# One packed operand for the last half block of a shared expert's gate and up projections

## The reference

```python
F, FS = (176, 704)
shared = silu(x @ Wsg) * (x @ Wsu) @ Wsd        # Wsg, Wsu: 256 x 704, Wsd: 704 x 256
shared = shared * jax.nn.sigmoid(x @ Wse)
...
out = shared.at[tok].add(y_pair)
```

## Time and profile before

| | us |
|---|---|
| median of three runs | 497.82 |
| the profiled execution | 498.43 |
| its span in the trace | 496.7 |
| TensorE busy in the span | 470.5 (95%) |
| VectorE busy | 288.1 (58%) |
| ScalarE busy | 212.9 (43%) |
| GpSimd busy | 57.4 (12%) |

### The profile page before, as it was taken

One profiled execution on the slowest core, in us unless ns is written; L12 is line 12 of the kernel. 1 busy time (PEld: TensorE's weight loads), 2 busy tenths in 40 slices (PEclk: granted clock), 3 DMA queues, 4 the chain that ended last, 5 costly groups with the idle time before them and its releaser, 6 DMA issues.

```text
span 496.7 us, 8113 instructions
## 1 busy us (share of the span) xinstructions
PE 470.5 (95%) x3022; PEld 393.2 (79%) x3022; DVE 288.1 (58%) x713; ACT 212.9 (43%) x564; POOL 57.4 (12%) x91
## 2 busy tenths in 40 slices
PE   1999999899999999999999989999989899999997
PEld 1778888798888889898989779899866656557897
DVE  5536553656666666666666655665688853535111
ACT  3454630355555556555555666334253232231100
POOL 4050000000000000000000000011432168400000
PEclk9999999999999999999999999999999999999999
DMA  7900520101010010100000000000599159910001
GB/s 197 235 14 1 170 74 11 43 1 44 0 40 6 3 41 2 42 1 1 2 1 1 1 1 1 1 1 1 178 297 296 45 155 278 300 29 1 1 32 54
DMA packets 40439, 32.33 MB, mean 65 GB/s; under 512 B 6432, under 2 KB 38864, under 8 KB 40400
## 3 DMA queue, kind: packets, MB, share of 16 engines
q1 hardware_dynamic: 40400, 31.80, 23.2%
HBM read 30.75 MB, written 1.05 MB: 64 GB/s over the span
## 4 chain that ended last, share of the span: by engine, by line
PE 78%; DVE 11%; ACT 5%; issue 3%; DMA 1%; POOL 0%; SPq 0%; ACTq 0%; DVEq 0%; POOLq 0%
PE bank L771 13%; PE bank L772 12%; PE bank L773 12%; PE bank L913 4%; PE bank L1133 4%; PE bank L930 4%; PE bank L921 3%; PE bank L947 2%; PE bank L1105 2%; PE bank L931 2%; ACT arena L611 2%; PE bank L911 2%; PE bank L1064 2%; PE bank L1125 2%; PE bank L1171 2%
## 5 line engine op out<-in xcount | busy, mean ns | idle before, releaser
L609 ACT ACTIVATE arena<-bank,nmax 128x128 f32<-128x128 f32 x64 | 23.5, 368 | 92.6 <-DVE nmax L1315 92.6
L771 PE MATMUL bank<-XTl,WA 128*128 128x512 f32 x128 | 54.7, 427 | 4.4 <-DVE XTl L1218 3.6
L772 PE MATMUL bank<-XTh,WA 128*128 128x512 f32 x128 | 51.4, 402 | 0.0
L773 PE MATMUL bank<-XTh,WA 128*128 128x512 f32 x128 | 51.4, 401 | 0.0
L489 POOL TENSOR_TENSOR arena<-arena 128x256 f32<-128x256 f32 x20 | 16.7, 862 | 278.5 <-ACT arena L672 258.4
L1320 DVE RECIPROCAL rinv<-psumr 128x2 f32<-128x2 f32 x64 | 10.6, 166 | 61.1 <-ACT arena L611 60.9
L913 PE MATMUL bank<-arena 128*128 128x256 f32 x128 | 41.6, 407 | 0.0
L771 PE MATMUL bank<-WA,XTh 128*128 128x256 f32 x128 | 38.4, 300 | 0.0
L930 PE MATMUL bank<-arena 128*128 128x256 f32 x128 | 38.3, 381 | 0.0
L921 PE MATMUL bank<-ident,arena 128*128 128x128 f32 x192 | 32.5, 278 | 5.7 <-DVE arena L1323 5.7
L772 PE MATMUL bank<-WA,XTl 128*128 128x256 f32 x128 | 35.7, 279 | 0.0
(11 more groups left out here) (261 smaller groups left out, 1219.0 us busy)
## 6 DMA issues: line engine op xcount, KB each, us to landing
arena<-in_L_ffn_Wg SPq DMA_DIRECT2D x6, 704.0 KB, 8.4
arena<-in_L_ffn_Wu SPq DMA_DIRECT2D x6, 704.0 KB, 9.8
arena<-in_L_ffn_Wd SPq DMA_DIRECT2D x6, 512.0 KB, 7.5
arena<-in_L_attn_Wq SPq DMA_DIRECT2D x4, 512.0 KB, 6.5
arena<-in_L_attn_Wk SPq DMA_DIRECT2D x8, 256.0 KB, 2.7
arena<-in_L_attn_Wv SPq DMA_DIRECT2D x8, 256.0 KB, 3.2
arena<-in_L_attn_Wo SPq DMA_DIRECT2D x1, 2048.0 KB, 8.3
arena<-in_L_ffn_Wd SPq DMA_DIRECT2D x6, 192.0 KB, 8.0
```

Source lines behind the costliest of these rows:

```text
L609: nc.scalar.activation(Pb[:, i, 0:128], pb[i][:, 0:128], ACT.Exp, bias=nmax[:, i, 0:1], accum_out=psumr[:, i, 0:1])
L771: pe.matmul(dst, wh, xl, start=start, stop=False)
L772: pe.matmul(dst, wl, xh, start=False, stop=False)
L773: return pe.matmul(dst, wh, xh, start=False, stop=stop)
```

## The change

The half blocks of gate and up, 64 columns each, are laid side by side in one operand of 128 columns (`tail`), high and low. For block 5 `shared_up` runs once for both (k = 0 alone; with k = 1 only its waits are left), and its one bank holds the gate's result in partitions 0 to 63 and the up projection's in 64 to 127. `silu` reads the lower half and writes to partitions 64 to 127 of `ACTT[5]`; `shared_product` multiplies there. The last 64 rows of the down weights are loaded to partitions 64 to 127, and `shared_down` multiplies block 5 with those 64 rows only. With no padding left, its two memsets and their semaphores go; the DMAs that waited for them wait for what the memsets waited for. `SGR` has 704 columns for each part and no gap.

```diff
-        SGR = region(9728, 3072).rearrange("p (a c n) -> p a c n", a=2, c=C)
+        SGR = region(9728, 4 * FS).rearrange("p (a c n) -> p a c n", a=2, c=C)
...
+        def tail(part):
+            return SG[:, (FC - 1) % 2, part, 0].rearrange("p c (a n) -> p a c n", a=2)
...
-            sp.wait_ge(s_pd, 1)
+            sp.wait_ge(s_ol, 2 * NT)
...
-                    sp.wait_ge(s_ps, 1)
+                    sp.wait_ge(s_yh, 2 * NT)
...
-                    sp.dma_start(SD[0:FS - P * (FC - 1), FC - 1], a["L1_ffn_Wsd"][P * (FC - 1):FS, :]).then_inc(s_sd, 16)
+                    sp.dma_start(SD[P - FT:P, FC - 1], a["L1_ffn_Wsd"][P * (FC - 1):FS, :]).then_inc(s_sd, 16)
...
             pool.wait_ge(s_ol, 2 * NT)
-            pool.memset(SGR[:, :, :, FS:FP], 0.0).then_inc(s_pd, 1)
...
             pool.wait_ge(s_yh, 2 * NT)
-            pool.memset(SD[:, FC - 1], 0.0).then_inc(s_ps, 1)
...
             def g_high(m):
...
+                if m == FC - 1:
+                    nc.scalar.activation(tail(0), SGR[:, :, :, P * m:FS], ACT.Copy).then_inc(s_gh, 1)
...
             def silu(q):
...
+                if m == FC - 1:
+                    nc.scalar.activation(ACTT[m][P - FT:P, 512 * half:512 * half + 512], pb[up_bank(q)][0:FT], ACT.Silu).then_inc(s_ss, 1)
+                    return
...
             def shared_up(q, k):
...
+                if m == FC - 1:
+                    if k == 0:
+                        for c in range(C):
+                            ins = mm3(pb[up_bank(q)][:], SG[:, m % 2, 0, 0, c], SG[:, m % 2, 1, 0, c],
+                                      XTh[:, c, xs], XTl[:, c, xs], c == 0, c == C - 1)
+                        ins.then_inc(s_sf, 2)
+                    return
...
             def shared_down(j):
...
-                    ins = pe.matmul(pb[j % 4][:, 0:D], ACTT[m][:, P * j:P * j + P], SD[:, m], start=(m == 0), stop=(m == FC - 1))
+                    r = slice(P - FT if m == FC - 1 else 0, P)
+                    ins = pe.matmul(pb[j % 4][:, 0:D], ACTT[m][r, P * j:P * j + P], SD[r, m], start=(m == 0), stop=(m == FC - 1))
...
             def g_low(m):
...
+                if m == FC - 1:
+                    for i in range(2):
+                        ins = nc.vector.tensor_tensor(tail(1)[:, i], SGR[:, i, :, P * m:FS], tail(0)[:, i].bitcast(F32), ALU.subtract)
+                    ins.then_inc(s_gl, 1)
+                    return
...
             def shared_product(q):
...
+                if m == FC - 1:
+                    nc.vector.tensor_tensor(dst[P - FT:P], dst[P - FT:P], pb[up_bank(q)][P - FT:P], ALU.mult).then_inc(s_sm, 1)
+                    return
```

More of the change, by code:

```diff
@@ L43 @@
 FC = 6
-FP = FC * P
+FT = FS - P * (FC - 1)
 SLOTS = E1 * CAP
@@ L262, in program @@
         s_x1 = sem("x1_ready")
-        s_pd = sem("shared_up_padding_ready")
-        s_ps = sem("shared_down_padding_ready")
         s_pe = sem("expert_padding_ready")
@@ L400, in _ @@
                 load_kv(p)
-            sp.wait_ge(s_pd, 1)
+            sp.wait_ge(s_ol, 2 * NT)
             for i, n in enumerate(("Wsg", "Wsu")):
-                sp.dma_start(SGR[:, i, :, 0:FS], a["L1_ffn_" + n].rearrange("(c p) n -> p c n", p=P)).then_inc(s_sg, 16)
+                sp.dma_start(SGR[:, i], a["L1_ffn_" + n].rearrange("(c p) n -> p c n", p=P)).then_inc(s_sg, 16)
             sp.wait_ge(s_pe, 3)
@@ L676, in g_high @@
                     act.wait_ge(s_sf, 2 * shared.index((m - 2, 1)) + 2)
-                nc.scalar.activation(SG[:, m % 2, 0], SGR[:, :, :, P * m:P * m + P], ACT.Copy).then_inc(s_gh, 1)
+                if m == FC - 1:
+                    nc.scalar.activation(tail(0), SGR[:, :, :, P * m:FS], ACT.Copy).then_inc(s_gh, 1)
+                else:
+                    nc.scalar.activation(SG[:, m % 2, 0], SGR[:, :, :, P * m:P * m + P], ACT.Copy).then_inc(s_gh, 1)
             o_high(3)
```

## The result

The changed kernel takes 502.85 us (median of 6 runs, 501.84 to 505.45) against 497.78 us; the ratio is 1.0102 with a 95% interval of 1.0079 to 1.0124, so it is 5.1 us slower. The direction was forecast, the size was not: 500.4 us was predicted, with a range from 498.7 to 501.5.

A forecast was written before the change was run, and what follows sets the result against it. TensorE, busy 470.5 of 496.7 us, was taken as the bound, with VectorE holding `shared_down`. Terms -0.56 and +3.2 gave +2.6 us: 500.4 us on the median of 497.82, range 498.7 to 501.5.

The forecast's parts named there:

- The bound: TensorE bounds the kernel, but from 446.73 to 449.23 us VectorE's copy, masks and last product hold `shared_down`.
- the up pass of q 11: Six multiplications removed behind `down` 7; they ended before VectorE's last shared product began, so removal gains 0.
- The turn of the last group, 0.56 us: In `turn` 7 the second transpose starts 0.22 us behind VectorE's product, at 443.42 instead of 443.98: gain 0.56 us.
- VectorE's part, 2.50 us "and it stays": From the start of the copy of `down` 7 to `shared_down`, VectorE's work stays 2.50 us long.
- The switches, 3.2 us: In `shared_down`, sixteen changes between 128 and 64 rows cost 0.20 us each, adding 3.2 us.
- four early distances: Early trace rows where the used array part changes: each load comes 0.07 us before the record ahead's modelled end.
- rivals of free and of half-priced switches: `shared_down`'s row switches cost nothing (497.3 us, chance 0.07) or half (498.8 to 498.9 us, chance 0.06).
- The memsets, "0": Removing both padding memsets, at 352.38 us and on an idle GpSimd, gains 0; without cover 0.3 us each at most.
- The clock, left out of the sum, chance 0.05: Rival: about 2.5 us idle ahead of `shared_down` halves TensorE's rate for 3.4 us, costing 1.7 more: 502.1, chance 0.05.
- 1.32 us of idle time: TensorE's idle stretch ahead of 393.64 us, after which its row shows full rate; cited when weighing the clock rival.

The follow-up runs named there:

- e7: Kernel before, both passes kept, only the up pass of q 11 moved ahead of `down` 7: 496.79 us against 497.55, ratio 0.9982.
- e10: Changed kernel without the waits that the two dropped passes left on TensorE's queue: 504.6 us, one run.
- e1: Changed kernel, but `shared_down` multiplies block 5 with all 128 rows (zeros added): 498.73 us against 498.21 before, ratio 1.0015.
- e3: Changed kernel plus six unused multiplications filling TensorE's idle stretch ahead of `shared_down`: 501.94 us, ratio 1.0076 to the kernel before.
- e6: Changed kernel with the edits of e1, e4 and e10 together: 493.98 us against 497.55 before, ratio 0.9927.
- e8: e1 plus the six unused multiplications of e3 in the idle stretch: 497.63 us, ratio 0.9999 to the kernel before.
- e12: Changed kernel plus two tiny early GpSimd memsets of 8 unused columns each: 501.66 us, one run.
- e2: Kernel before, both up passes kept, only `shared_down` changed to multiply block 5 with rows 0 to 63: 501.24 us against 498.21, ratio 1.0067.
- e9: e4 with `shared_down`'s blocks descending for every second j, so 8 row switches instead of 16: 496.8 us against 497.94 before, ratio 0.997.
- e5: Changed kernel plus one GpSimd memset of 64 unused rows where the second padding memset was: 501.78 us, ratio 1.0079 to the kernel before.
- e11: Changed kernel plus one tiny early GpSimd memset of 8 unused columns: 502.08 us, one run.
- e4: Changed kernel with both packed passes of block 5 written ahead of `down` 7: 498.05 us, ratio 0.9998 to the kernel before.

## Why the prediction was wrong

*The bound.* Right: VectorE held `shared_down`, and the up pass of q 11 was worth nothing. e7 confirms it from the other side.

*The turn of the last group, 0.56 us.* The mechanism held, the size did not. The product ended at 443.94 and the second transpose started at 444.33, 0.39 us later and not 0.22. The waits of the dropped pass stay on TensorE's queue and are worked off only behind the product; in e10, without them, it is 0.22 (one run). The prediction put no price on them.

*VectorE's part, 2.50 us "and it stays".* It became 449.87 - 447.13 = 2.74. Before, the mask began 0.34 us behind the start of the copy and before the copy's end (VectorE's timeline; the chain in the earlier trace rows shows the time from the copy's end on):

```profile
447.07 1.41 DVE L1529 TENSOR_SCALAR GT<-FRF,slot_t 128x1024 fp32r<-128x1024 f32 x2
```

Now the mask begins 0.46 us behind it, when the copy is over, and the product waits for the end of the masks (447.59 + 1.42 = 449.01, then 449.04), where before it began 0.09 us ahead of it. The copy and the mask are 0.45 or 0.46 us apart in every trace of a kernel with the product in partitions 64 to 127, whatever the order and the rows of `shared_down` (e1, e3 to e6, e8 to e12), and 0.34 in the traces of those without (e2, e7), and in the changed kernel itself at 440.33, before the first such product. So it goes with the 64-partition product; whether its size or its place does it was not tried. With the turn, this leaves 0.10 us of the 0.56.

*The switches, 3.2 us.* Right: 3.09 in e2, 0.19 each, and half of them half the price in e9. (Of the four early distances that the prediction read as the same 0.07, one, 18.85 to 18.77, is 0.08.) The rivals of free and of half-priced switches fall. The Trainium skill's sentence on the drain (TensorEngine Tiling (Array Packing), Key Properties) agrees with all of these rows.

*The memsets, "0".* The memsets' own time was covered, but without both of them the stretch around 392 us takes 0.46 us more and has an idle stretch of 2.01 us (e5, e11, e12). The sum had this at nothing.

*The clock, left out of the sum, chance 0.05.* This is the step that failed. The rival was named, with its place and its price: 1.7 us more, 502.1. The traces measure 1.69 (e1) and 1.64 (e11, e12) for a fall of some 3.4 us. The chance was wrong: behind an idle stretch of 2.81 us the clock fell in 5 of 7 runs of the changed kernel, 6 of 12 of e1, 2 of 6 of e5, and in the single runs of e10, e11 and e12: 16 of 28. I had taken full rate behind 1.32 us of idle time as evidence for 2.5, where no row spoke; that needed a chance near one half, and a range that reached 503. The Trainium skill, TensorE: Matmul & The Clock Gate, Why this matters for your kernels, warns of idle gaps between bursts of multiplications, because the clock falls back behind them. The trace agrees, but the gap that the page names is longer than the 2.81 us that were enough here in half of the runs, and the measurement decides.

Put together, the median was missed by 2.45 us: 1.64 for a fall of the clock, 0.46 at 392 us, and 0.46 of the 0.56 us of gain that did not arrive, less 0.11 for the switches. From the other side, 3.09 for the switches, 0.46 at 392 us, less 0.10, plus 1.64 is 5.09 us, and 5.07 was measured. That the two agree so closely is partly luck. The two runs at clock 1.000 (501.84 and 502.62) lie 4.1 and 4.8 us above before where 3.45 is explained, and both are outside the forecast's range without any fall of the clock; the four at 0.996 average 502.86, only 0.63 above these two. By whole runs a fall thus seems to cost 0.6 to 0.8 us here and in e1, where the traces show 1.64 to 1.69; what offsets the rest is not known. Part of the scatter arises early: TensorE's transposes behind the 1.57 us stretch, far ahead of anything that the change touches, start anywhere from 97.13 us (e12) to 99.03 (e9), and the kernel before spreads from 496.65 to 498.95 in one job.

The profiled run lost 3.29 us to the clock, twice as much as e1, because the low clock lasted 6.8 us. e10 did the same; e1, e11 and e12 had 3.4 us. With 64-row switches both lengths occur, and the mean clock tells them apart (0.993, and 0.996 or 0.997). What decides between them is open.

## What to carry to other kernels

Work taken from the busiest engine is worth only what it delayed: look at what stands behind each removed piece, and move something there before counting the gain (e6 against the changed kernel; it also has 128 rows and no left-over waits). An operand cut to 64 rows in the midst of full ones cost two switches of 0.19 us here and saved nothing; zeros are cheaper, or such pieces belong side by side. A removed cover also lengthens an idle stretch, and at 2.0 to 2.8 us the clock of TensorE became part of the price in some runs and not in others, so it belongs into the sum with a chance.

## What the runs showed of the hardware that was not expected

The clock does not fall in every run of a kernel, and the longer idle stretch goes with the higher share. With a longest stretch (after the first 20 us) of 2.81 us it fell in 16 of 28 runs; with 2.01 us in 5 of 29 (e3 2 of 6, e4 1 of 12, e9 2 of 11); with 1.57 us in none of 36 (e2, e6, e7, e8) and in none of 63 runs of the kernel before. A mean clock of 0.997 or less is counted as a fall. That the stretch is the cause was tested for the 2.81 us alone (e8); for the 2.01 us it is one trace (e3) and the counts.

With 89 instructions on GpSimd in place of 90 or 91, however small and however early the added ones are, its start behind a wait of over 12 us is 0.35 us later, and TensorE's wait for what hangs on it goes from 1.3 to 2.0 us. No run shows the cause.

VectorE's operations around a product in partitions 64 to 127 do not overlap as they did before: from the copy to the mask 0.46 us in place of 0.34, from the masks to the product 1.45 in place of 1.32, and from the product to the next operation 0.72 in place of 0.60. Each starts when the one ahead is over.
